# Retention's first tiles: block 1 copied and scaled a tile later, output weights' low half at tile 2, weight splits spread over more tiles

## The chip, the cores and the metric

The kernel runs on one NeuronCore of a Trainium2 chip. The metric is the device time of one execution in microseconds (us), the median over several executions; smaller is better. The core has five engines that run side by side and meet at semaphores: TensorE (PE, matrix products and transposes), VectorE (DVE), ScalarE (ACT), GpSimd (POOL) and SyncE (SP), which here only issues transfers.

## The reference

The reference is a chain of four residual blocks on x of shape (2, 2048, 256), that is 4096 rows of 256 values:

```python
x = x + _L0_attn_a_ref(_layernorm(x, axis=-1), ...)   # retention + ffn, two layers
x = x + _L0_ffn_ref(_layernorm(x, axis=-1), w_up, w_down)
x = x + _L0_attn_b_ref(_layernorm(x, axis=-1), ...)   # window attention
x = x + _L0_ffn_ref(_layernorm(x, axis=-1), w_up, w_down)
```

The change touches the first block alone, and in it the retention of each of the two layers:

```python
for i in range(L):                                     # L = 2
    Xn = _layernorm(X, ln1_w[i], ln1_b[i])
    Q = jnp.einsum('bsd,hdk->bhsk', Xn, WQ[i])
    K = jnp.einsum('bsd,hdk->bhsk', Xn, WK[i])
    V = jnp.einsum('bsd,hdk->bhsk', Xn, WV[i])
    Q = Q * cosq + _rotate_every_two(Q) * sinq
    K = K * cosk + _rotate_every_two(K) * sink
    scores = jnp.einsum('bhsk,bhtk->bhst', Q, K) * Dm[None]
    Yh = jnp.einsum('bhst,bhtk->bhsk', scores, V)
    Y = Yh.transpose(0, 2, 1, 3).reshape(B, S, H * HD)
    Y = _groupnorm(Y, gn_w[i], gn_b[i])
    G = jax.nn.silu(Xn @ WG[i])
    Y = G * Y @ WO[i] + X
    Yn = _layernorm(Y, ln2_w[i], ln2_b[i])
    X = jax.nn.silu(Yn @ ffn_w1[i] + ffn_b1[i]) @ ffn_w2[i] + ffn_b2[i] + Y
```

## The kernel before

The program is a row of stages: `retention` (layer 0), `ffn`, `retention` (layer 1), `ffn`, a ternary ffn, the window attention, and a ternary ffn. x stays in SBUF the whole time. Every product is made of fp32 halves: a matrix w is split into w_hi, a copy in fp32r that ACT makes (`high_half`, L79), and w_lo = w - w_hi, which DVE makes (`low_half`, L85), and a product is three passes (hi x hi, hi x lo, lo x hi).

`retention` works on 32 tiles n of 128 rows. Four tiles are a block b of 512 rows; blocks alternate between the two batch entries. Each engine has a body that is written out by hand, in which turn k of iteration i issues a few steps, each on another tile or block, so the order of an engine's work is the order of the code. Iteration i = 0 holds what comes ahead of the first tile; in iteration i = 1 turn k is tile n = k. The iterations 0, 1 and the last two are written out, the others are one loop. `at_start(x)` is true where x is the number 0, so `at_start(n)` is tile 0, `at_start(n - 1)` tile 1 and `at_start(n - 2)` tile 2. The argument `first` is set in layer 0 alone: there x and all weights have to be loaded first, and the input of the layer is itself normalised in place (`rows_in_place` on ACT, with scales from `scale_in_place` on POOL).

For one tile n the steps are these. TensorE makes the products for queries and keys (`project_heads`, tile pj), DVE turns them (`rotate`, L1337 and L1340), POOL adds the two parts (`rotary_sum`, L1233), TensorE transposes them (`transpose_heads`, L1783), and ACT copies that out (`heads_out`, L1567). Then come the scores (L1798), one tile later in the order; DVE masks them (`masked`, L1350), and TensorE makes the new state and the outputs (`chunk_out`, L1811 to L1822). DVE carries the state on (`next_state`, L1366 to L1371), ACT copies the outputs (`columns_out`, L1578), TensorE transposes them back, and ACT copies the rows (`rows_out`, L1585). The scores of tile n + 1 wait for all of these: for the state sum (`in_done`), for `columns_out` of tile n (`y_moved`) and for `rows_out` of tile n - 1 (`y_done`), since they share one PSUM tile, sc.

For a block the normalised rows are transposed (L1773), ACT copies them as xt and xt_hi (`inputs`, L1560), and DVE makes xt_lo (`input_low`, L1326). Of block 1 the first half of this, `inputs(1, 0, 1)` and `input_low(1, 0, 1)`, is done in tiles 1 and 2.

The weights of the ffn that follows are loaded during retention. SP issues two transfers of 1 MB into the tile staging, `loads`, with the semaphore `prefetched`. In layer 0 staging holds the layer's own weights until then, so SP first waits for all five of their low halves, of which `own_low(4)`, the output weights', is the last:

```python
                sp.wait_ge(own_lo_done, len(first["halves"]))
            prefetch(sp, loads, prefetched)
```

Eight jobs (`halves`, four for the up weights, four for the down weights) then split them: ACT makes a high half, and DVE waits for it (`hi_done`) and makes the low one. Before, both did two jobs at the end of each of the tiles 4 to 7.

Of the kernel before, what the change touches and what calls it, by code (L numbers as in the profile page):

```python
# [107 lines left out]
def at_start(idx):  # L108

    return isinstance(idx, int) and idx == 0  # L110
# [895 lines left out]
def retention(nc, name, X, ident, lane, *, qkv, gate, out_w, norm, gn, rotary, decay, group_eps, carry, state_decay,  # L1006
# [8 lines left out]
    with ExitStack() as c:  # L1015
# [98 lines left out]
        U = 2 * TB  # L1114
# [5 lines left out]

        TOTAL = NB + (next_norm is not None)

        def transposed(b, j):

            return tr[0] if first is not None and at_start(b) and j == 1 else tr[1]
# [32 lines left out]
        def _(pool):  # L1158
# [92 lines left out]
            def body(i):  # L1251
                for k in range(U):
                    n = U * i + k - AHEAD
                    if live(n, NT):
                        rotary_sum(n, k)
                    if k % TB == TB - 1 and fresh(2 * i + k // TB):
                        if not at_start(i):
                            scales(2 * i + k // TB, k // TB)
                        elif k == TB - 1:
                            first_scale(0)  # L1260
                            scale_in_place(0)
                    if at_start(n):
                        first_scale(1)
                        if first is not None:
                            scale_in_place(1)
                    if isinstance(i, int) and i == N and k == U - 1:
                        second_scale()
                    at = (k - AHEAD - 4) // 2
                    if k % 2 == 0 and live(4 * i + at, NH):
                        group_rstd(4 * i + at, at)  # L1270
                    at = (k - AHEAD - 5) // 2
                    if k % 2 == 1 and live(4 * i + at, NH):
                        gated(4 * i + at, at)
# [4 lines left out]
        def _(dve):  # L1278
# [36 lines left out]
            def aggregate(b, at):  # L1315
                at_least(dve, xn_done, b - 1)
                dve.wait_ge(stats_done, TB * (b + 1))
                apart(dve, dve_waited)
                for t in range(TB):
                    last = nc.vector.bn_aggr(mv[:, at % 2, t, :], stats[:, t, :])  # L1320
                last.then_inc(mv_done, 1)
# [138 lines left out]
            def body(i):  # L1460
                if isinstance(i, int) and i == N + 1:
                    drain(i)
                    return
                for k in range(U):
                    n = U * i + k - AHEAD
                    if first is not None and at_start(n):
                        dve.wait_ge(rotary_loaded, 16 * 2)
                    if live(n, NT):
                        rotate(n, i, k - AHEAD)
                    if first is not None and at_start(n - 1):  # L1470
                        dve.wait_ge(tables_loaded, 16 * (len(first["tables"]) - 2))
                    if live(n - 1, NT):
                        masked(n - 1, k - 1)
                    if live(n, NT):
                        values(n, k)
                    if at_start(n):
                        for t in range(TB):
                            statistics(1, 0, 1, t)
                        aggregate(1, 1)
                        if first is not None:  # L1480
                            own_low(4)
                    if at_start(n - 1):
                        first_normalise(1)
                    if k % 2 == 0:
                        at = (k - AHEAD - 4) // 2
                        if live(4 * i + at, NH):
                            square_sums(4 * i + at)
                        at = (k - AHEAD - 6) // 2
                        if live(4 * i + at, NH):
                            gated_low(4 * i + at)  # L1490
                    else:
                        at = (k - AHEAD) // TB + 1
                        if fresh(2 * i + at):
                            input_low(2 * i + at, k % TB // 2, at)
                        if first is not None and at_start(i) and k == U - 1:
                            own_low(2)
                            own_low(3)
                        at = (k - AHEAD - 7) // 2
                        if live(4 * i + at, NH):
                            residual(4 * i + at, i, at)  # L1500
                    if live(n - 1, NT):
                        next_state(n - 1, k - 1)
                    if at_start(i) and k >= TB:
                        pass
                    elif fresh(2 * i + k // TB) or (after_last(2 * i + k // TB) and i == N):
                        if k % TB < TB - 1:
                            statistics(2 * i + k // TB, i, k // TB, k % TB)
                        if k % TB == TB - 2:
                            statistics(2 * i + k // TB, i, k // TB, TB - 1)
                            aggregate(2 * i + k // TB, k // TB)  # L1510

                    if at_start(i) and k == TB - 2:
                        if first is not None:
                            first_normalise(0)
                            for j in range(2):
                                own_low(j)
                            centre_values()
                        dve.wait_ge(consts_set, 3)
                    if isinstance(i, int) and i == 1 and k >= U // 2:
                        for j in range(2 * k - U, 2 * k - U + 2):  # L1520
                            dve.wait_ge(hi_done, j + 1)
                            low_half(nc, halves[j])

# [7 lines left out]
        def _(act):  # L1531
# [116 lines left out]
            def body(i):  # L1648
# [3 lines left out]
                for k in range(U):  # L1652
                    n, t = U * i + k - AHEAD, k % TB
                    b, at = 2 * i + (k - AHEAD) // TB, (k - AHEAD) // TB
                    if live(n - 2, NT):
                        columns_out(n - 2, k - 2)
                    q = 4 * i + (k - AHEAD - 3) // 2
                    if live(n - 3, NT):
                        rows_out(n - 3, q, k - AHEAD - 3)
# [28 lines left out]
                            normed(4 * i + half)  # L1688
                    if live(n, NT):
                        heads_out(n, k)  # L1690
                    if at_start(n - 1):
                        inputs(1, 0, 1)
                    if at_start(i) and k == TB - 1 and first is not None:
                        act.wait_ge(qkv_loaded, 16)
                        own_high(0)
# [4 lines left out]
                    if first is not None and at_start(n):  # L1700
                        act.wait_ge(weights_loaded, 16 * (len(first["weights"]) - 2))
                        own_high(4)
                        act.wait_ge(tables_loaded, 16 * (len(first["tables"]) - 2))
                    if isinstance(i, int) and i == 1 and k >= U // 2:
                        if k == U // 2:
                            act.wait_ge(prefetched, 16 * len(loads))
                        for j in range(2 * k - U, 2 * k - U + 2):
                            high_half(nc, halves[j]).then_inc(hi_done, 1)

            if first is not None:  # L1710
# [1146 lines left out]
```

## Time and profile before

| | us |
|---|---|
| median of 3 timed runs | 1497.44 (1497.07 to 1497.51) |
| the profiled execution | 1497.22 |
| its span, first to last instruction | 1495.3 |
| busy: PE, DVE, ACT, POOL | 1431.2, 1035.8, 929.8, 831.9 |

The profile's page gives busy times of each engine, shares of 40 slices of the span, the transfers, the chain of work that ended last and the costliest groups of instructions. The trace behind it gives each instruction with its start, its length, the idle time of its engine before it and what ended that. All rows shown here are of the one profiled execution.

### The profile page before, as it was taken

What the parts mean: (1) busy time and instruction counts of PE and PEld (TensorE: products, weight loads), DVE (VectorE), ACT (ScalarE), POOL (GpSimd) and SP (SyncE); (2) the same over time, 40 slices, a digit from 0 to 9 for tenths busy, and PEclk for the clock granted to TensorE, in tenths of its full rate; (3) what the DMA queues carried; (4) which work ended last, traced back from release to release, by engine and by line L of the source; (5) the groups of instructions that cost most, each with busy time, mean ns of one, the idle gap of its engine ahead of it and who ended that gap; (6) DMA issues with size and microseconds to landing.
All of it is one profiled execution on the core that took longest, in us unless ns stands there. A gap on an engine that the chain in (4) does not pass through costs nothing. (4 is left out here: it accounts for less than half of the span.)

```text
span 1495.3 us, 36363 instructions
## 1 busy us (share of the span) xinstructions
PE 1431.2 (96%) x13034; PEld 1188.7 (79%) x13066; DVE 1035.8 (69%) x2284; ACT 929.8 (62%) x1748; POOL 831.9 (56%) x915
## 2 busy tenths in 40 slices
PE   5999999999998999999999999997999999989998
PEld 4777878899986788878999888885777777768886
DVE  6878777564537877885755678665777777756774
ACT  4665565565544555555655567775777777758775
POOL 3665766411204676573824457766666676636674
PEclk9999999999999999999999999999999999999999
DMA  7000000100001000000210010000000000000101
GB/s 250 2 2 1 0 2 2 36 1 1 1 15 44 2 2 0 1 1 34 95 29 15 1 40 2 0 1 1 2 1 0 0 0 0 0 2 1 42 30 43
DMA packets 21143, 26.27 MB, mean 18 GB/s; under 512 B 1952, under 2 KB 19104, under 8 KB 20896
## 3 DMA queue, kind: packets, MB, share of 16 engines
q1 hardware_dynamic: 20736, 24.61, 5.0%
q8 instruction: 75, 1.23, 0.3%
q14 instruction: 44, 0.36, 0.1%
q10 hardware_dynamic: 288, 0.07, 0.0%
HBM read 20.48 MB, written 4.19 MB: 17 GB/s over the span
## 5 line engine op out<-in xcount | busy, mean ns | idle before, releaser
L547 DVE TENSOR_TENSOR ffn_h_lo<-ffn_h,ffn_h_hi 128x512 fp32r<-128x512 f32 x112 | 86.2, 770 | 122.2 <-ACT ffn_h_hi L754 122.2
L753 ACT ACTIVATE ffn_h<-ffn_hp,c_b 128x512 f32<-128x512 f32 x112 | 77.2, 689 | 145.3 <-PE ffn_hp L850 144.8
L547 DVE TENSOR_TENSOR ternary_ffn_h_lo<-ternary_ffn_h,ternary_ffn_h_hi 128x512 fp32r<-128x512 f32 x128 | 110.8, 866 | 76.0 <-ACT ternary_ffn_h_hi L754 75.7
L1233 POOL TENSOR_TENSOR ret_qk<-ret_qk,ret_qk_sin 128x512 f32<-128x512 f32 x64 | 82.7, 1292 | 103.2 <-DVE ret_qk_sin L1340 102.6
L861 PE MATMUL ternary_ffn_yp<-down_ternary,ternary_ffn_h_hi 128*128 128x256 f32 x512 | 132.3, 291 | 0.0
L1239 POOL TENSOR_TENSOR ret_rstd<-ret_sums,ret_minus_half 128x16 f32<-128x16 f32 x32 | 103.7, 3240 | 42.7 <-DVE ret_sums L1382 42.7
L861 PE MATMUL ffn_yp<-down_hi,ffn_h_hi 128*128 128x256 f32 x448 | 127.4, 284 | 0.0
L861 PE MATMUL ternary_ffn_yp<-down_ternary,ternary_ffn_h_lo 128*128 128x256 f32 x512 | 127.4, 280 | 0.0
L861 PE MATMUL ffn_yp<-down_hi,ffn_h_lo 128*128 128x256 f32 x448 | 125.0, 279 | 0.0
L861 PE MATMUL ffn_yp<-down_lo,ffn_h_hi 128*128 128x256 f32 x448 | 124.9, 279 | 0.0
L443 POOL TENSOR_TENSOR ternary_ffn_h_sq<-ternary_ffn_h_sq 128x512 f32<-128x512 f32 x61 | 94.6, 1560 | 41.9 <-ACT ternary_ffn_h_sq L760 38.2
L2179 POOL TENSOR_TENSOR win_rms<-win_rms,win_minus_half 128x20 f32<-128x20 f32 x31 | 115.3, 3718 | 2.6
L2403 ACT ACTIVATE wa_probs_t<-wa_tp 128x512 f32<-128x512 f32 x128 | 76.4, 597 | 62.7 <-PE wa_tp L2580 62.2
L753 ACT ACTIVATE ternary_ffn_h<-ternary_ffn_hp 128x512 f32<-128x512 f32 x128 | 76.5, 597 | 54.1 <-PE ternary_ffn_hp L850 47.8
L850 PE MATMUL ternary_ffn_hp<-xt_hi,up_ternary 128*128 128x512 f32 x256 | 102.4, 400 | 4.7 <-DVEq L730 4.4
L861 PEld LDWEIGHTS ternary_ffn_yp<-down_ternary,ternary_ffn_h_hi 128*128 128x128 f32 x512 | 96.4, 188 | 7.3 <-issue 3.8
L850 PE MATMUL ternary_ffn_hp<-xt_lo,up_ternary 128*128 128x512 f32 x256 | 101.6, 397 | 0.0
L861 PEld LDWEIGHTS ternary_ffn_yp<-down_ternary,ternary_ffn_h_lo 128*128 128x128 f32 x512 | 96.6, 189 | 3.1
L1337 DVE TENSOR_TENSOR ret_qk<-ret_pj,rotary 128x512 f32<-128x512 f32 x64 | 44.2, 690 | 68.7 <-PE ret_pj L1729 68.7
L850 PE MATMUL ffn_hp<-xt_hi,up_hi 128*128 128x512 f32 x224 | 88.9, 397 | 2.4 <-DVEq L730 2.4
L850 PE MATMUL ffn_hp<-xt_lo,up_hi 128*128 128x512 f32 x224 | 88.9, 397 | 0.0
L1350 DVE TENSOR_TENSOR ret_probs<-ret_sc,causal 128x1024 f32<-128x1024 f32 x64 | 78.3, 1224 | 15.0 <-issue 10.9
(322 smaller groups left out, 4700.2 us busy)
## 6 DMA issues: line engine op xcount, KB each, us to landing
staging<-in_w SPq DMA_DIRECT2D x4, 1024.0 KB, 7.0
ffn_x_in<-in_x SPq DMA_DIRECT2D x8, 512.0 KB, 3.9
X<-in_x SPq DMA_DIRECT2D x7, 512.0 KB, 7.9
out<-X SPq DMA_DIRECT2D x7, 512.0 KB, 2.9
staging<-in_wqkv SPq DMA_DIRECT2D x2, 768.0 KB, 5.7
rotary<-in_rotary SPq DMA_DIRECT2D x1, 1024.0 KB, 7.3
staging<-in_w_up SPq DMA_DIRECT2D x1, 1024.0 KB, 5.0
staging<-in_w_down SPq DMA_DIRECT2D x1, 1024.0 KB, 7.5
```

The source lines that it names most:

```text
L443: nc.gpsimd.tensor_tensor(h_sq[:, m, :], h_sq[:, m, :], h_sq[:, m + 1, :], ALU.add).then_inc(sq_added, 1)
L547: nc.vector.tensor_tensor(h_lo[:, m % R, :], h[:, m % R, :], h_hi[:, m % R, :].bitcast(F32), ALU.subtract).then_inc(h_ready, 1)
L753: nc.scalar.activation(h[:, m % R, :], hp[m % 2][:, :], fn, bias=bias)
L850: last = nc.tensor.matmul(hp[m % 2][:, :], w[:, j, m * P:(m + 1) * P], x[:, k, j, :], start=(n == 0), stop=(n == len(todo) - 1))
L861: last = nc.tensor.matmul(yp[k][t // 2][:, (t % 2) * D:(t % 2 + 1) * D], x[:, m % R, t * P:(t + 1) * P], w[:, m, :], start=(m == 0 and t % ...
L1233: nc.gpsimd.tensor_tensor(qk[:, r, :, :, :], qk[:, r, :, :, :], qk_sin[:, r, :, :, :], ALU.add).then_inc(qk_done, 1)
L1239: nc.gpsimd.tensor_tensor(rstd[:, :], sums[:, 1, :], minus_half[:, :], ALU.pow).then_inc(rstd_done, 1)
L1337: nc.vector.tensor_tensor(qk[:, r, :, :, :], src, cos, ALU.mult)
L1350: nc.vector.tensor_tensor(pr[:, at % 2, :, :, :], sc[:, :, 0:HT].rearrange("p h (j n) -> p h j n", j=NG), causal[:, :].unsqueeze(1).unsque ...
L2179: nc.gpsimd.tensor_tensor(rms[:, 1, :], rms[:, 0, :], minus_half[:, :], ALU.pow).then_inc(rms_work, 1)
L2403: nc.scalar.activation(pt[:, g, :, :].rearrange("p c n -> p (c n)"), tp[:, :], ACT.Copy).then_inc(pt_done, 1)
```

## The change

Three edits, all in `retention`, and all in the written-out iteration i = 1 (tiles 0 to 7):

1. `scale_in_place(1)` on POOL goes from tile 0 to tile 1, behind the rotary sum; `inputs(1, 0, 1)` on ACT goes from the end of tile 1 to tile 2, behind `columns_out(0)`; `input_low(1, 0, 1)` on DVE goes from tile 1 to tile 2, behind the values.
2. `own_low(4)` on DVE goes from tile 0 to tile 2, behind that `input_low`.
3. The eight jobs are spread by `split_at`: in layer 0 two at tile 2, one each at 3 and 4, two at 5, one each at 6 and 7; in layer 1 one at each of the tiles 0 to 7.

The steps of TensorE and SP keep their order.

```diff
+        def split_at(k):
+
+            if first is None:
+                return (k,)
+            return {2: (0, 1), 3: (2,), 4: (3,), 5: (4, 5), 6: (6,), 7: (7,)}.get(k, ())
...
                     if at_start(n):
                         first_scale(1)
-                        if first is not None:
-                            scale_in_place(1)
+                    if at_start(n - 1) and first is not None:
+                        scale_in_place(1)
...
-                        if first is not None:
-                            own_low(4)
                     if at_start(n - 1):
                         first_normalise(1)
+                    if at_start(n - 2):
+                        input_low(1, 0, 1)
+                        if first is not None:
+                            own_low(4)
...
-                        if fresh(2 * i + at):
+                        if fresh(2 * i + at) and not at_start(n - 1):
                             input_low(2 * i + at, k % TB // 2, at)
...
-                    if isinstance(i, int) and i == 1 and k >= U // 2:
-                        for j in range(2 * k - U, 2 * k - U + 2):
+                    if isinstance(i, int) and i == 1:
+                        for j in split_at(k):
                             dve.wait_ge(hi_done, j + 1)
                             low_half(nc, halves[j])
...
                         columns_out(n - 2, k - 2)
+                    if at_start(n - 2):
+                        inputs(1, 0, 1)
...
-                    if at_start(n - 1):
-                        inputs(1, 0, 1)
...
-                    if isinstance(i, int) and i == 1 and k >= U // 2:
-                        if k == U // 2:
+                    if isinstance(i, int) and i == 1:
+                        if split_at(k) and split_at(k)[0] == 0:
                             act.wait_ge(prefetched, 16 * len(loads))
-                        for j in range(2 * k - U, 2 * k - U + 2):
+                        for j in split_at(k):
                             high_half(nc, halves[j]).then_inc(hi_done, 1)
```

In the pieces of each engine's order below, the line numbers of the changed kernel are 6 (DVE) and 8 (ACT) higher. DVE in layer 0, from the end of tile 0 to the rotation of tile 2, before:

```order
L85 TENSOR_TENSOR out_w_lo<-staging,out_w_hi 128x512 [waits ret0_own_hi_done]
L1312 BN_STATS ret_stats<-X 128x6 [waits ret0_x_loaded2,ret0_mv_done]
L1337 TENSOR_TENSOR ret_qk<-ret_pj,rotary 128x512 [waits ret0_qk_full]
L1340 TENSOR_TENSOR ret_qk_sin<-ret_pj,rotary 128x256 x2
L1350 TENSOR_TENSOR ret_probs<-ret_sc,causal 128x1024 [waits ret0_v_full,ret0_sc_full,ret0_tables_loaded]
L1358 TENSOR_TENSOR ret_v<-ret_sc,decay 128x256 [waits ret0_v_full]
L1406 TENSOR_SCALAR xn<-X,mean_var,ret_scale 128x256 [waits ret0_tp_full,ret0_first_scaled]
L1406 TENSOR_SCALAR xn<-X,mean_var,ret_scale 128x256 x3
L1326 TENSOR_TENSOR xt_lo<-xt,xt_hi 128x512 [waits ret0_xt_read]
L1366 TENSOR_TENSOR ret_state_in<-ret_sc,ret_own_state 128x64 [waits ret0_kv_full]
```

and in the changed kernel, DVE of layer 0 from the mask of tile 2's turn (that of tile 1) to the rotation of tile 3:

```order
L1356 TENSOR_TENSOR ret_probs<-ret_sc,causal 128x1024 [waits ret0_v_full,ret0_sc_full]
L1364 TENSOR_TENSOR ret_v<-ret_sc,decay 128x256 [waits ret0_y_full,ret0_v_full]
L1332 TENSOR_TENSOR xt_lo<-xt,xt_hi 128x512 [waits ret0_xt_read]
L85 TENSOR_TENSOR out_w_lo<-staging,out_w_hi 128x512 [waits ret0_own_hi_done]
L1372 TENSOR_TENSOR ret_state_in<-ret_sc,ret_own_state 128x64 [waits ret0_state_done,ret0_kv_full]
L1375 TENSOR_TENSOR ret_own_state<-ret_state_in,carry 128x64 [waits ret0_in_done]
L1377 TENSOR_TENSOR ret_state<-ret_state_in,state_decay 128x256
L1318 BN_STATS ret_stats<-X 128x6 x2
L1326 BN_AGGR mean_var<-ret_stats 128x2 [waits ret0_xn_done,ret0_stats_done]
L85 TENSOR_TENSOR up_lo<-staging,up_hi 128x512 [waits ret0_hi_done] x2
L1343 TENSOR_TENSOR ret_qk<-ret_pj,rotary 128x512 [waits ret0_kv_full,ret0_qk_full]
```

xt_lo and out_w_lo have moved behind the values of tile 2, and two low halves of the up weights stand ahead of the rotation of tile 3. ACT of layer 0 in the changed kernel, from the gates of tile 2 to the copy of the next inputs:

```order
L1581 ACTIVATE ret_gate<-ret_pj 128x512 [waits ret0_g_full]
L1575 ACTIVATE ret_qkt<-ret_tr 128x512 [waits ret0_y_full,ret0_tq_full]
L79 ACTIVATE up_hi<-staging 128x512 [waits ret0_prefetched]
L79 ACTIVATE up_hi<-staging 128x512
L1586 ACTIVATE ret_y_cols<-ret_sc 128x256 [waits ret0_y_full]
L1593 ACTIVATE ret_y<-ret_sc 128x256 [waits ret0_back_full]
```

Before, the two rows of up_hi stood two tiles further on, behind the copy of tile 4's heads, and with them the wait for prefetched. DVE of layer 1 in the changed kernel, at the end of tile 0 (hi_done is the count of high halves):

```order
L85 TENSOR_TENSOR up_lo<-staging,up_hi 128x512 [waits ret0_hi_done]
L1343 TENSOR_TENSOR ret_qk<-ret_pj,rotary 128x512 [waits ret0_pool_waited]
L1346 TENSOR_TENSOR ret_qk_sin<-ret_pj,rotary 128x256 x2
```

The low half stands ahead of the rotation of tile 1, where nothing stood before. (Layer 1 uses the semaphores of layer 0 again under other meanings, and the order prints the first name that each had.)

## Rows read from the trace of the kernel before

**Rows 1.** The page, part 1: busy us, share, instructions of each engine.

```profile
PE 1431.2 (96%) x13034; PEld 1188.7 (79%) x13066; DVE 1035.8 (69%) x2284; ACT 929.8 (62%) x1748; POOL 831.9 (56%) x915
```

**Rows 2.** Timeline of PE, layer 0: start, length, instruction [idle before, releaser].

```profile
20.99 0.39 PE L1729 MATMUL ret_pj<-qkv_hi,xt_lo 128*128 128x512 f32 x1
...
25.05 0.66 PE L1783 MATMUL ret_tr<-c_ident,ret_qk 128*128 128x128 f32 x4 [2.11 <-POOL ret_qk L1233]
...
30.26 0.73 PE L1798 MATMUL ret_sc<-ret_qkt 32*128 32x128 f32 x16 [1.08 <-DVE ret_state_in L1366]
...
31.61 0.28 PE L1729 MATMUL ret_sc<-qkv_hi,xt_lo 128*128 128x256 f32 x1
...
37.56 0.73 PE L1798 MATMUL ret_sc<-ret_qkt 32*128 32x128 f32 x16
...
40.42 0.66 PE L1783 MATMUL ret_tr<-c_ident,ret_qk 128*128 128x128 f32 x4 [1.24 <-POOL ret_qk L1233]
```

**Rows 3.** Timeline of DVE and POOL, layer 0, tiles 0 to 2.

```profile
21.16 0.69 DVE L85 TENSOR_TENSOR out_w_lo<-staging,out_w_hi 128x512 fp32r<-128x512 f32 x1 [1.11 <-ACT out_w_hi L79]
...
22.11 0.67 DVE L1337 TENSOR_TENSOR ret_qk<-ret_pj,rotary 128x512 f32<-128x512 f32 x1
...
29.29 0.69 DVE L1326 TENSOR_TENSOR xt_lo<-xt,xt_hi 128x512 fp32r<-128x512 f32 x1 [3.10 <-ACT xt_hi L1560]
...
32.22 1.22 DVE L1350 TENSOR_TENSOR ret_probs<-ret_sc,causal 128x1024 f32<-128x1024 f32 x1
33.35 0.41 DVE L1358 TENSOR_TENSOR ret_v<-ret_sc,decay 128x256 f32<-128x256 f32 x1
...
23.73 1.27 POOL L1233 TENSOR_TENSOR ret_qk<-ret_qk,ret_qk_sin 128x512 f32<-128x512 f32 x1
32.38 1.29 POOL L1233 TENSOR_TENSOR ret_qk<-ret_qk,ret_qk_sin 128x512 f32<-128x512 f32 x1 [7.38 <-DVE ret_qk_sin L1340]
```

**Rows 4.** Timeline of DVE, layer 0: the rotation of tile 3.

```profile
37.67 0.69 DVE L1337 TENSOR_TENSOR ret_qk<-ret_pj,rotary 128x512 f32<-128x512 f32 x1 [0.95 <-PE ret_pj L1729]
```

**Rows 5.** Timelines of DVE and PE, layer 1, tiles 1 and 2.

```profile
452.31 0.69 DVE L1337 TENSOR_TENSOR ret_qk<-ret_pj,rotary 128x512 f32<-128x512 f32 x1 [0.89 <-PE ret_pj L1729]
...
453.55 0.28 PE L1729 MATMUL ret_sc<-qkv_hi,xt_lo 128*128 128x256 f32 x1
455.06 0.66 PE L1783 MATMUL ret_tr<-c_ident,ret_qk 128*128 128x128 f32 x4 [1.23 <-POOL ret_qk L1233]
...
460.27 0.73 PE L1798 MATMUL ret_sc<-ret_qkt 32*128 32x128 f32 x16 [1.08 <-DVE ret_state_in L1366]
```

**Rows 6.** SP's issues, and issue to landing of the second load, layers 0 and 1.

```profile
21.88 0.89 SPq L68 DMA_DIRECT2D staging<-in_w  x2
...
DMA to landing us min/median/max: 8.8/8.8/8.8
...
445.55 0.88 SPq L68 DMA_DIRECT2D staging<-in_w  x2
...
DMA to landing us min/median/max: 7.5/7.5/7.5
```

**Rows 7.** Timeline of ACT, layer 0.

```profile
35.92 0.39 ACT L1578 ACTIVATE ret_y_cols<-ret_sc 128x256 f32<-128x256 f32 x1 [0.91 <-PE ret_sc L1822]
...
48.92 1.14 ACT L79 ACTIVATE up_hi<-staging 128x512 fp32r<-128x512 f32 x2
```

**Rows 8.** PE at the window stage; a slice: length, busy PE, PEld, DVE, ACT, POOL, clock.

```profile
1021.10 0.45 PE L2529 MATMUL wa_tr<-c_ident,win_padded 128*128 128x128 f32 x1 [3.83 <-DVEq L2213]
...
1021.00:1024.00 3.00, 2.90 (x11) 2.74 (x11) 1.90 (x5) 2.14 (x4) 0.98 (x4) 0.50 0.03 5
```

**Rows 9.** Timelines of POOL and PE at the end of tile 7.

```profile
67.15 1.29 POOL L1233 TENSOR_TENSOR ret_qk<-ret_qk,ret_qk_sin 128x512 f32<-128x512 f32 x1 [0.43 <-DVE ret_qk_sin L1340]
...
76.59 0.65 PE L1773 MATMUL ret_tr<-c_ident,xn 128*128 128x128 f32 x4 [1.23 <-ACT xn L1536]
...
505.97 0.65 PE L1773 MATMUL ret_tr<-c_ident,xn 128*128 128x128 f32 x4 [0.62 <-ACT xn L1536]
```

More of the change, by code:

```diff
@@ L1479, in body @@
                         aggregate(1, 1)
+                    if at_start(n - 1):
+                        first_normalise(1)
+                    if at_start(n - 2):
+                        input_low(1, 0, 1)
                         if first is not None:
                             own_low(4)
-                    if at_start(n - 1):
-                        first_normalise(1)
                     if k % 2 == 0:
@@ L1690, in body @@
                         heads_out(n, k)
-                    if at_start(n - 1):
-                        inputs(1, 0, 1)
                     if at_start(i) and k == TB - 1 and first is not None:
```

## The prediction

> **What bounds the kernel now.** I read the page first, then the timelines of the four engines, TensorE's first, through the first tiles of each retention layer, since only there does the change act. The page shows TensorE busy for 96% of the span [rows 1]; so the end is set by TensorE's own queue: a microsecond of its idle time that is removed or added stays until the end, unless it is given back at a later wait. TensorE's waits in layer 0's first tiles are few: for the rotary sum on POOL (2.11 us in tile 1, 1.24 in tile 3), and once for DVE's state sum, 1.08 us at the scores of tile 1 [rows 2]. These are what the change can win. What it can lose is the slack of ACT and DVE: both work in order, so one wait at a tile's end holds everything of the next tile.
>
> I call the layers 0 and 1, tiles n = 0, 1, 2, and "scores(n)" and so on by the names of the code. A start at 37.56 means us from the span's start.
>
> **Part 1, layer 0: the output weights' low half (own_low(4)) leaves tile 0.** Before, DVE waited 1.11 us for ACT's copy and then spent 0.69 us on it; rotate(1) could only start at 22.11, and POOL's sum, behind scale_in_place(1), started at 23.73 [rows 3]. The product that rotate(1) reads ended at 21.38 (20.99 + 0.39). A clean rotate starts about 0.04 us after its product, and takes 2.75 us to the transposes of its heads: 37.67 to 40.42 in tile 3, 452.31 to 455.06 in layer 1 [rows 2, 4, 5]. With scale_in_place(1) put behind POOL's sum, the transposes of tile 1 start at 21.42 + 2.75 = 24.17 instead of 25.05 [rows 2]: 0.88 us won. DVE has no work of another kind to put in that hole, so nothing replaces it. scale_in_place(1) now runs behind that sum, where POOL stood idle for 7.38 us [rows 3], and ACT asks for its result only behind the inputs' copy: hidden.
>
> **Part 2, both layers: input_low(1, 0) moves to tile 2, behind the values.** DVE stood 3.10 us at it, with the state sum behind, and TensorE's scores(1) waited 1.08 us for that sum [rows 2, 3]. Now the state sum runs before, and the inputs' copy on ACT runs behind columns_out(0), which the same scores need. Won: 1.08 us in each layer. The low half itself (0.69 us) lies in DVE's slack ahead of the state sum of tile 1, and nothing reads it before tile 4.
>
> So far layer 0 is 1.96 us ahead: scores(2) could start at 37.56 - 1.96 = 35.60 [rows 2].
>
> **Part 3, layer 0: the weight splits start at tile 2, but their loads now start later.** This is the term that decides. SP issues the two loads of 1 MB when the fifth low half is done (it overwrites the same staging tile). Before, that was at 21.88, right behind own_low(4) [rows 3, 6]. Now own_low(4) stands behind the mask, the values and input_low(1, 0) of tile 2. The values' product ends at 31.61 + 0.28 - 1.96 = 29.93 [rows 2]; the mask then takes 1.22, the values 0.41, the two low halves 0.69 each [rows 3], with about 0.1 us of overlap at each handover: 32.8. The second load is issued 0.4 us later, at 33.2. Its time to landing was 8.8 us here, right behind the blocks of x, and 7.5 us in layer 1 with the queue empty [rows 6]. At tile 2 the queue is empty, so I take 7.5 and keep 8.8 as the upper bound: landed at 40.8 (42.1).
>
> ACT now waits for that at the end of tile 2, from about 33.0, where before it asked at 48.92, long after the landing [rows 7]. Behind the wait on ACT stand the two high halves (1.14), columns_out(1) (0.39) and rows_out(0) (0.4) [rows 7], and TensorE's scores(2) wait for both of the last: 40.8 + 1.9 - 0.1 = 42.6 instead of 35.6. TensorE stands for 7.0 us. DVE stands too: its low halves 0 and 1 wait for the high halves, the last ends at 42.7, and only then comes rotate(3), which was at 37.67 [rows 4]. Its transposes follow at 42.7 + 2.75 = 45.4, against 40.42: 5.0 us late.
>
> **The clock after such a stand.** At the start of the window stage TensorE was idle for 3.83 us, and the granted clock was 0.50 right after, that is 1.2 instead of 2.4 GHz, over the 3 us from 1021 to 1024 [rows 8]. A stand of 7.0 us is longer. So scores(2) and the values' product of tile 3, 1.6 us of work at full clock, take about 2.8; the mask of tile 2 starts at 45.4 and ends at 46.6, and chunk_out(2), which came 0.6 us behind the transposes at 41.0 before, starts at 46.65. The step at tile 2 is +5.6 us with the low clock, +5.0 without.
> The Trainium skill (TensorE: Matmul & The Clock Gate, Part 1) says that an idle array falls back to 1.2 GHz and returns to 2.4 GHz after sustained work; by that rule the trace agrees, and the larger of the two values stands.
>
> A weighing of the load itself: the second load ended 7.9 us after the first was issued in layer 1 [rows 6].
> The Trainium skill (DMA: Bandwidth & Descriptors, Rules for kernel authors) wants a transfer issued early and waited for late, which is what this change undoes; its fit in Anatomy of one DMA (2.0 us and the bytes at 436 GB/s, given there for another issuing path) would give an estimate of 6.8 us for both loads, and the sum would be 1.1 us lower by it.
>
> **Part 4, layer 1: the first half at tile 0.** Here the loads are issued at 445.55 when the layer starts, and the second lands at 445.55 + 0.4 + 7.5 = 453.5 [rows 6]. ACT now waits for it behind heads_out(0); that costs ACT nothing, its next step waits for the transposes of tile 1. But DVE's low_half(0) stands ahead of rotate(1): high half to 454.1, low half to 454.8, and rotate(1) starts then instead of at 452.31 [rows 5]: +2.5 us for the transposes of tile 1 (455.06). Part 2 gives 1.08 back at scores(1) (460.27) [rows 5]. Left: +1.4 us.
>
> **Part 5, the splits at one per tile.** In tiles 4 to 7 DVE and ACT carry half of what they did where one split stands for two. TensorE waits for none of them, so most of it is worth nothing. One place counts: POOL's sum of tile 7 waited 0.43 us for a rotate that came behind two low halves, and TensorE's transposes of the following block waited 1.23 us (layer 0) and 0.62 us (layer 1) for a chain that runs through that sum [rows 9]. I take 0.4 us in each layer; bounds 0 and 0.6.
>
> **The sum.** Layer 0: +5.6 - 0.4 = +5.2. Layer 1: +1.4 - 0.4 = +1.0. Together +6.2 us. The profiled execution took 1497.2 us (span 1495.3), 0.2 us below the median of 1497.4 of the timed runs. 1497.4 + 6.2 = **1503.6 us**. A measurement of this kernel tells about 0.2% from no change, 3.0 us.
>
> **The rivals.**
> 1. *The second stand also lowers the clock.* In layer 1 TensorE would be idle from 453.83 to 457.55, 3.7 us; the row that shows a fall had 3.83, and the 2.11 us in layer 0 brought none: the transposes behind it took 0.66 us as in tile 3 [rows 2]. Three us at 0.50 are 1.5 us of work lost [rows 8], nearly all of it on the path: 1505.1 us.
> 2. *The loads land as slowly as before (8.8 us):* +1.3, 1504.9 us. For it: the same two transfers once took that. Against: x is all in by then.
> 3. *The clock stays up, or ACT's chain is a little shorter:* 1503.0 us.
> 4. *Later slack gives half of it back.* TensorE's remaining waits in the layers are for chains that hang on TensorE's own work and shift with it, which speaks against: 1500.5 us.
> 5. *Not slower: ACT's wait is hidden.* If the loads had landed when ACT asks, layer 0 would keep its 1.96 and 0.4 us, with layer 1 at +1.0: 1496.1 us. The point from which it decides: columns_out(1) is due on ACT at 35.92 - 1.96 = 33.96 [rows 7], less 1.14 for the high halves, so the landing has to come by 32.8, the moment of its issue. No load of 1 MB landed in under 5.0 us. Were the wait of layer 1 hidden as well, 1493.6 us.
>
> **How the numbers follow.** Forecast 0.52, rival 1 0.20, rival 2 0.10, rival 3 0.08, rival 4 0.06, rival 5 0.04 (of which 0.02 with both waits hidden). The range: rivals 1 and 2 together would be 1503.6 + 1.5 + 1.3 = 1506.4; below, rival 3 and the bound of 0.6 in part 5 with 1 us less of load give 1501.6. Low 1501.6, high 1506.5. Slower by over 0.2% (above 1500.4): everything but half of rival 4, and rival 5: 0.93. Within 0.2%: 0.05. Faster: 0.02.
>
> **What would show it.** Right: ACT's up_hi in layer 0 starts near 40.8 with some 7 us of idle time before it, released by the DMA; scores(2) start near 42.6 with a wait for ACT's ret_y; the granted clock is 0.5 in the three us that follow; the scores(1) rows have no wait for ret_state_in in either layer; the first transposes of tile 1 are near 24.2 and 457.5. Wrong: up_hi starts before 36, or scores(2) near 35.6; or tile 8 of layer 0 is less than 4 us later than before.

## The result and the profile after

| | before, us | changed, us |
|---|---|---|
| median of 5 timed runs | 1497.07 (1495.22 to 1497.51) | 1504.94 (1503.05 to 1506.66) |
| the profiled execution | 1497.22 | 1506.66 |
| its span | 1495.3 | 1504.9 |

The ratio is 1.0051, with an interval of 1.0039 to 1.0062: the changed kernel is slower. The median moved by 7.9 us (1504.94 - 1497.07), the span of the two profiled executions by 9.6 (1504.9 - 1495.3). Beside [rows 1], the page of the changed kernel has the same instructions in the same number, but for matmul records that one trace or the other lost:

```profile
PE 1441.4 (96%) x13066; PEld 1195.2 (79%) x13066; DVE 1036.4 (69%) x2284; ACT 930.9 (62%) x1748; POOL 829.8 (55%) x915
```

DVE, ACT and POOL are as busy as before. TensorE's busy time is 10.2 us larger with the same work (before, 32 matmul records are missing): matmuls that ran at the lower clock are longer ones. The line numbers of the changed kernel are 6 (DVE, POOL) and 8 (ACT, PE) higher than before.

**The waits.** TensorE's three longest groups of waits, on the page's trace (waits for: us in total, times, longest):

```profile
PE ret_tr L1781 <- DVE xn L1412: 9.1, 1, 9.1
PE ret_tr L1791 <- POOL ret_qk L1239: 8.5, 6, 3.6
PE ret_sc L1806 <- ACT ret_y L1593: 8.3, 3, 7.2
```

The first is the kernel's start and stands in both (9.9 us before). The third is new: the scores wait for ACT, once for 7.2 us. The longest of the second group, 3.6 us, is new too and lies in layer 1.

**Layer 0.** TensorE's timeline, answering to [rows 2]:

```profile
23.29 0.66 PE L1791 MATMUL ret_tr<-c_ident,ret_qk 128*128 128x128 f32 x4 [1.23 <-POOL ret_qk L1239]
...
30.66 0.60 PE L1791 MATMUL ret_tr<-c_ident,ret_qk 128*128 128x128 f32 x4
...
41.68 1.24 PE L1806 MATMUL ret_sc<-ret_qkt 32*128 32x128 f32 x16 [7.17 <-ACT ret_y L1593]
...
44.46 1.11 PE L1791 MATMUL ret_tr<-c_ident,ret_qk 128*128 128x128 f32 x4
...
54.78 0.60 PE L1791 MATMUL ret_tr<-c_ident,ret_qk 128*128 128x128 f32 x4
```

The wait at tile 1's transposes fell from 2.11 to 1.23 us, the wait for ret_state_in at its scores is gone, and in their place scores(2) stand for 7.17 us. Why is on SP's, ACT's and DVE's timelines, one after the other:

```profile
31.88 0.89 SPq L68 DMA_DIRECT2D staging<-in_w  x2
```

```profile
39.84 1.15 ACT L79 ACTIVATE up_hi<-staging 128x512 fp32r<-128x512 f32 x2 [7.95 <-DMA staging<-in_w]
40.89 0.36 ACT L1586 ACTIVATE ret_y_cols<-ret_sc 128x256 f32<-128x256 f32 x1
41.16 0.37 ACT L1593 ACTIVATE ret_y<-ret_sc 128x256 f32<-128x256 f32 x1
```

```profile
40.50 1.29 DVE L85 TENSOR_TENSOR up_lo<-staging,up_hi 128x512 fp32r<-128x512 f32 x2 [6.73 <-ACT up_hi L79]
41.71 0.68 DVE L1343 TENSOR_TENSOR ret_qk<-ret_pj,rotary 128x512 f32<-128x512 f32 x1
```

SP issues the two loads of 1 MB at 31.9, ten microseconds later than in [rows 6]; ACT asks for them at the end of tile 2 and stands for 7.95 us until the second has landed. The columns of tile 1 and the rows of tile 0 on ACT, for which the scores of tile 2 wait, and the rotation of tile 3 on DVE are queued behind the splits.

**Layer 1.** TensorE's, ACT's and DVE's timelines, answering to [rows 5]:

```profile
464.07 0.94 PE L1791 MATMUL ret_tr<-c_ident,ret_qk 128*128 128x128 f32 x4 [3.65 <-POOL ret_qk L1239]
...
469.56 0.73 PE L1806 MATMUL ret_sc<-ret_qkt 32*128 32x128 f32 x16
```

```profile
460.06 0.63 ACT L79 ACTIVATE up_hi<-staging 128x512 fp32r<-128x512 f32 x1 [1.95 <-DMA staging<-in_w]
```

```profile
460.72 0.69 DVE L85 TENSOR_TENSOR up_lo<-staging,up_hi 128x512 fp32r<-128x512 f32 x1 [2.68 <-ACT up_hi L79]
461.33 0.68 DVE L1343 TENSOR_TENSOR ret_qk<-ret_pj,rotary 128x512 f32<-128x512 f32 x1
```

The wait for ret_state_in is gone here too, but ACT waits 1.95 us for the load, rotate(1) runs behind the low half of the first split, and the transposes of tile 1 stand for 3.65 us.

**The clock.** Slices of TensorE's granted clock in the changed kernel, around the two stands (length of the slice, busy time of PE, PEld, DVE, ACT, POOL with their counts, then the clock as a share of 2.4 GHz, DMA share, GB/s):

```profile
34.00:38.00 4.00, 0.51 (x3) 0.07 (x1) 0.00 (x0) 0.00 (x0) 0.00 (x0) 0.95 1.04 398
38.00:45.00 7.00, 3.32 (x25) 2.87 (x26) 2.97 (x6) 3.03 (x6) 1.69 (x3) 0.50 0.18 58
45.00:46.00 1.00, 0.71 (x13) 0.31 (x15) 1.00 (x2) 0.39 (x1) 0.93 (x1) 0.50 0.00 0
46.00:51.00 5.00, 5.00 (x43) 3.84 (x42) 2.04 (x6) 2.95 (x7) 1.30 (x3) 0.50 0.00 0
51.00:52.00 1.00, 1.00 (x18) 0.53 (x16) 0.42 (x1) 1.00 (x3) 0.00 (x0) 0.85 0.00 0
...
464.00:468.00 4.00, 3.93 (x45) 2.89 (x45) 3.14 (x10) 1.50 (x3) 0.02 (x1) 0.57 0.00 0
```

It fell to 1.2 GHz during the first stand, and was back only in the slice from 51 to 52, some 9.6 us after the scores had started (41.68). In layer 1 it fell as well, to 0.57 on average over four microseconds.

**Where the time went.** Start of the transposes of a tile's heads on TensorE, counted from those of the layer's tile 0 (the changed kernel's layer 0 started 0.89 us earlier, at 18.43 against 19.32, which is no effect of the change: the same start lies between 18.4 and 19.3 over the profiled executions of all runs here). The columns "late" are the differences:

| | before | changed | late, us |
|---|---|---|---|
| layer 0, tile 1 | 5.73 | 4.86 | -0.87 |
| tile 2 | 14.40 | 12.23 | -2.17 |
| tile 3 | 21.10 | 26.03 | +4.93 |
| tile 4 | 28.23 | 36.35 | +8.12 |
| tile 8 | 57.76 | 65.25 | +7.49 |
| layer 1, tile 1 | 4.85 | 7.25 | +2.40 |
| tile 2 | 13.52 | 16.05 | +2.53 |
| tile 8 | 56.25 | 58.12 | +1.87 |

Together +7.49 + 1.87 - 0.89 = +8.5 of the 9.6 us; the rest is at the starts of later stages, which the change doesn't touch (last section).

### The profile page after: what moved, and what is told of

It is laid out like the page before. It is cut to its first block and busy times, and to the rows that moved or that the text cites. A ratio compares the mean times of both kernels' runs of the same rounds, so it can differ in the third digit from the quotient of the medians.

```text
span 1504.9 us, 36395 instructions
## 1 busy us (share of the span) xinstructions
PE 1441.4 (96%) x13066; PEld 1195.2 (79%) x13066; DVE 1036.4 (69%) x2284; ACT 930.9 (62%) x1748; POOL 829.8 (55%) x915
## 3 DMA queue, kind: packets, MB, share of 16 engines
q8 instruction: 75, 1.23, 0.3%
```

## The experiments

Each was timed beside the kernel before on the same chip. The kernel before had a median of 1498.51 us beside the first four, and 1498.19 beside the next four. The ratio is estimated from all of these runs and differs from the quotient of the two medians by up to 0.0006, 0.9 us. The edits are shown against the changed kernel. "Late" is used as in the table above, and "early" for the opposite.

**Both other edits, the splits where they were.** Edits 1 and 2 of the change alone (the copies a tile on, own_low(4) at tile 2); all splits from tile 4 in both layers:

```
         def split_at(k):
 
-            if first is None:
-                return (k,)
-            return {2: (0, 1), 3: (2,), 4: (3,), 5: (4, 5), 6: (6,), 7: (7,)}.get(k, ())
+            return {4: (0, 1), 5: (2, 3), 6: (4, 5), 7: (6, 7)}.get(k, ())
```

> Edits 1 and 2 alone: both layers' splits two per tile from tile 4 as before. Theory: 1.96 us won in layer 0 and 1.08 us in layer 1, nothing lost: 3.0 us under the kernel before, 1494.0 us. Rival (the late loads or the moved copies cost something): same as before or slower.

Measured: 1494.53 us, ratio 0.9973 (0.9963 to 0.9982): faster. Tile 8 of layer 0 is 2.26 us early, tile 2 of layer 1 1.30 us early, and the scores of tile 2 don't wait. TensorE's timeline:

```profile
34.50 0.73 PE L1804 MATMUL ret_sc<-ret_qkt 32*128 32x128 f32 x16
37.35 0.66 PE L1789 MATMUL ret_tr<-c_ident,ret_qk 128*128 128x128 f32 x4 [1.23 <-POOL ret_qk L1237]
```

So the gains of the first two edits are real, and all of the loss belongs to the early splits or to their meeting with edit 2. The loads are issued late here as well, at 31.94; nobody asks for them before 45.85, when they are long in.

**Layer 0's splits late, layer 1's early.**

```
             if first is None:
                 return (k,)
-            return {2: (0, 1), 3: (2,), 4: (3,), 5: (4, 5), 6: (6,), 7: (7,)}.get(k, ())
+            return {4: (0, 1), 5: (2, 3), 6: (4, 5), 7: (6, 7)}.get(k, ())
```

> The change, but with layer 0's splits two per tile from tile 4 as before; own_low(4) stays in tile 2, so the loads stay late (issued near 32, landing near 40). Theory: nobody asks for them before tile 4's end near 45, so layer 0 wins its 1.96 us and no stand is left; layer 1 +2.1 us as in the change, near 1497.2 us. Rival (late loads cost in themselves, through SP or the queue): layer 0 stays slower, 1500 us or more.

Measured: 1497.1 us, 0.9995 (0.9986 to 1.0004). Layer 0 keeps its gain though its loads are issued at 32.09: tile 8 is 2.27 us early, so late loads that nobody asks for cost nothing there. Tile 2 of layer 1 is 3.39 us late, against 2.53 in the changed kernel's first profile: the clock was low there from about 454.2 to 461.0, twice as long as in the changed kernel.

**Layer 1's splits late, layer 0's early.**

```
             if first is None:
-                return (k,)
+                return {4: (0, 1), 5: (2, 3), 6: (4, 5), 7: (6, 7)}.get(k, ())
```

> The change, but with layer 1's splits two per tile from tile 4 as before. Theory: layer 1's stand of 3.65 us goes and its low clock with it, and 1.08 us are won there against the kernel before; layer 0 keeps its loss. About 3.3 us under the change: 1501.6 us. Rival (layer 1's low half ahead of rotate(1) is hidden): within 1 us of the change.

Measured: 1502.17 us, 1.0025 (1.0015 to 1.0035). Against both late, layer 0's early splits cost 1502.17 - 1494.53 = 7.6 us and layer 1's 1497.1 - 1494.53 = 2.6 us. The two costs stand apart, in the layers where the theory puts them. With the 4.0 us that splits_late wins (1498.51 - 1494.53) they make +6.2 us; the changed kernel's interval was +5.8 to +9.3 us (1.0039 to 1.0062).

**The same early splits, with the loads issued early.** Only own_low(4) goes back into tile 0:

```
                         aggregate(1, 1)
+                        if first is not None:
+                            own_low(4)
                     if at_start(n - 1):
                         first_normalise(1)
                     if at_start(n - 2):
                         input_low(1, 0, 1)
-                        if first is not None:
-                            own_low(4)
```

> The change, but with the output weights' low half (own_low(4)) back in tile 0; the splits stay spread from tile 2 (layer 0) and tile 0 (layer 1). Theory (the loads): SP issues the two loads near 21 again, they land near 30, before ACT asks near 32, so ACT has no wait, TensorE no stand and no low clock in layer 0. Layer 0 then keeps the 1.08 us at scores(1), some 0.2 us at tile 1 and 0.5 us at tile 8; layer 1 stays about 2.1 us slower than before. Together near 1497.4 us, 7 us under the change. Rival (the work): the high and low halves ahead of columns_out and of rotate in tiles 2 and 3 cost by themselves; then at least half of the loss of layer 0 stays, 1501 us or more.

Measured: 1498.85 us, 0.9997 (0.9988 to 1.0007), on the same chip and in the same runs as split1_late. The stand in layer 0 is gone although its splits are at tile 2, as in the change. SP's timeline, then ACT's, then TensorE's:

```profile
21.15 0.89 SPq L68 DMA_DIRECT2D staging<-in_w  x2
```

```profile
32.59 1.14 ACT L79 ACTIVATE up_hi<-staging 128x512 fp32r<-128x512 f32 x2
```

```profile
24.11 0.66 PE L1791 MATMUL ret_tr<-c_ident,ret_qk 128*128 128x128 f32 x4 [1.90 <-POOL ret_qk L1239]
...
35.24 0.73 PE L1806 MATMUL ret_sc<-ret_qkt 32*128 32x128 f32 x16
```

ACT finds the data there (the second load is issued at 21.6 and takes 8.1 us) and doesn't wait; scores(2) don't either. Tile 8 of layer 0 is 2.05 us early. What remains is layer 1's loss: tile 2 there is 2.72 us late. That settles the cause in layer 0: not the splits at tile 2, but their meeting with loads that edit 2 had put off by 10 us.

**Edit 1 alone** (the next block's rows a tile on; own_low(4) in tile 0, splits from tile 4).

> Edit 1 alone: scale_in_place(1), inputs(1, 0) and input_low(1, 0) moved, own_low(4) in tile 0 and the splits in tiles 4 to 7 as before. Theory: 1.08 us won in each layer at scores(1), and 0.2 us at tile 1 of layer 0, where POOL's sum no longer stands behind scale_in_place(1): 2.4 us under the kernel before, 0.6 us above edits 1 and 2 together. Rival (the 0.88 us at tile 1 belongs to POOL's order and not to own_low(4)): the same as edits 1 and 2 together.

Measured: 1496.49 us, 0.9985 (0.9976 to 0.9994); the medians differ by 1.7 us. Tile 1 of layer 0 is 0.21 us early, against 0.88 in splits_late, so the other 0.67 us belong to own_low(4) and the rival is out. (By time alone it isn't: the interval overlaps that of splits_late.) The gain at tile 2 of layer 0 can't be read from this profile: TensorE waited 1.96 us at the transposes of tile 1, the clock was at 0.50 from about 25.8 to 29.2, and tile 2 is neither early nor late. In layer 1, tile 2 is 1.31 us early (463.31 - 451.10 against 13.52).

**Keeping the clock up during the stand.** 27 products of 128x512 that nobody reads, ahead of the scores of tile 2, behind a wait that lets them start when the stand begins:

```
+                    if at_start(n - 3) and first is not None:
+                        pe.wait_ge(tq_done, 3)
+                        for _ in range(27):
+                            nc.tensor.matmul(tr[0][:, :], xt_hi[:, 0, 0, 0:P], qkv[0][:, 0, 0:2 * D], start=True, stop=True)
                     if live(n - 1, NT):
                         scores(n - 1, k - 1)
```

> The change, and during layer 0's stand TensorE makes 27 products of 128x512 that nobody reads (some 6.4 us of work, into the PSUM tile that the next head transposes overwrite), ahead of scores(2). Theory (the clock): the stand keeps its length and its wait for ACT, but the granted clock stays 1.00 behind it, so the transposes of tile 4 come 5.0 us late instead of 8.1, and the time falls by about 3 us under the change. Rival (the loss behind the stand is the chain DVE, POOL, ACT and not the clock): within 0.5 us of the change.

Measured: 1504.17 us, 1.0038 (1.0024 to 1.0052), single runs from 1501.04 to 1506.61. The profile shows what was meant: the clock stays at 1.00 and the scores take 0.73 us instead of 1.24, so that tile 4 is 4.82 us late, not 8.12. Slices, then TensorE:

```profile
34.00:38.00 4.00, 4.00 (x19) 3.22 (x18) 0.00 (x0) 0.00 (x0) 0.00 (x0) 1.00 1.03 392
38.00:45.00 7.00, 5.12 (x46) 3.76 (x47) 4.26 (x8) 3.04 (x6) 1.73 (x4) 1.00 0.17 55
```

```profile
41.57 0.73 PE L1806 MATMUL ret_sc<-ret_qkt 32*128 32x128 f32 x16 [0.73 <-ACT ret_y L1593]
```

The stand alone therefore costs its 4.8 us at tile 4 and after; what is above that is the clock. In time the gain is not shown: the interval takes in the lower part of the changed kernel's (1.0039 to 1.0062).

**The same in both layers**, with 12 such products ahead of the transposes of tile 1 in layer 1.

> As the run before, and 12 more such products (2.8 us) in layer 1 ahead of the head transposes of tile 1. Theory: the 3.65 us stand of layer 1 stays, its low clock goes; layer 1 is then 1.4 us slower than before instead of 2.5 (by the tile starts), 1.1 us under the run before.

Measured: 1502.28 us, 1.0027 (1.0018 to 1.0035). In layer 1 the clock stayed at 1.00, and tile 2 is 1.14 us late instead of 2.53: the stand without the clock. The interval lies below the whole of the changed kernel's (1.0039 to 1.0062, each beside the kernel before on its own chip): in time too, part of the loss is the clock. How much is left open, for in layer 0 the clock fell all the same, though TensorE had worked through the stand and since then never waited for more than 1.15 us. TensorE's waits there:

```profile
41.90 0.73 PE L1806 MATMUL ret_sc<-ret_qkt 32*128 32x128 f32 x16 [0.81 <-ACT ret_y L1593]
44.68 1.12 PE L1791 MATMUL ret_tr<-c_ident,ret_qk 128*128 128x128 f32 x4 [1.15 <-POOL ret_qk L1239]
```

and two of its slices:

```profile
45.00:46.00 1.00, 1.00 (x20) 0.67 (x18) 0.78 (x2) 0.16 (x1) 0.90 (x2) 0.50 0.00 0
46.00:51.00 5.00, 5.00 (x42) 3.71 (x32) 1.40 (x4) 3.31 (x8) 1.91 (x3) 0.50 0.00 0
```

warm_layer0 has the same instructions in layer 0 and nearly the same waits there (0.73 and 1.14 us), and its clock stayed at 1.00. I had no theory that expects this fall, and have none now.

**The splits as far apart as the loads allow.** From this, a version: edits 1 and 2 as they are, layer 0's first split at tile 4, layer 1's at tile 1:

```
             if first is None:
-                return (k,)
-            return {2: (0, 1), 3: (2,), 4: (3,), 5: (4, 5), 6: (6,), 7: (7,)}.get(k, ())
+                return {1: (0,), 2: (1,), 3: (2,), 4: (3,), 5: (4, 5), 6: (6,), 7: (7,)}.get(k, ())
+            return {4: (0, 1, 2), 5: (3, 4), 6: (5,), 7: (6, 7)}.get(k, ())
```

> Edits 1 and 2, and the splits spread where the loads have landed: layer 0 three at tile 4, two at 5, one at 6, two at 7; layer 1 one each at tiles 1 to 4, two at 5, one each at 6 and 7. Theory: no stand in either layer, and the single split at tile 6 gives back 0.4 to 0.5 us at tile 8 in each layer: 3.8 us under the kernel before, 0.8 us under edits 1 and 2 alone. Rival (three at tile 4 push ACT's copies into scores(5), or the gain at tile 8 is taken by the next wait there): no better than edits 1 and 2 alone.

Measured: 1493.76 us (1490.91 to 1494.14), 0.9964 (0.9951 to 0.9977): faster than the kernel before and the changed one. Its interval overlaps that of splits_late (0.9963 to 0.9982), so that the spreading in itself is worth anything is not shown in time. In the profile tile 8 is 0.37 us earlier than in splits_late in layer 0 (2.63 against 2.26 early) and 0.62 in layer 1 (1.98 against 1.36), as part 5 of the prediction has it.

**How long the low clock lasts.** In the first profiles of the change and of split1_late the stand was nearly the same (7.17 and 7.04 us; tile 3 is 4.93 and 4.73 us late), but tile 4 was 8.12 us late in one and 5.55 in the other. So two more executions of each were profiled.

> The changed kernel, one more execution. In its first profile the granted clock stayed at 0.50 from the stand to 51.2 us and tile 4 of layer 0 began 8.1 us late against tile 0; in split1_late, with the same layer 0, it was back by 45.2 us and tile 4 was only 5.5 us late. Theory (the stand is fixed, the length of the low clock behind it is settled anew in every execution): tile 3 again 4.9 to 5.0 us late, tile 4 either about 5.5 or about 8.1 us late, and over four looks both are seen. Rival (the length belongs to the kernel): 8.1 us in every look at this kernel.

> As changed_look2. Theory: tile 3 4.9 to 5.0 us late, tile 4 about 5.5 or about 8.1. Rival: 8.1. In layer 1 tile 2 is 2.5 us late where the clock falls behind the stand of 3.7 us, and 1.4 where it doesn't; my theory expects the fall in most looks, not in all.

> Split1_late (layer 1's splits from tile 4, layer 0 as in the change), one more execution. Theory: tile 3 of layer 0 4.9 to 5.0 us late, tile 4 about 5.5 or about 8.1. Rival (the length belongs to the kernel): 5.5 again.

> As split1_late_look2. Theory: tile 4 about 5.5 or about 8.1 us late. Rival: 5.5.

Measured, with the time of that execution (one execution of the kernel before took 1500.19 us on this chip):

| execution | us | tile 3 late | tile 4 late |
|---|---|---|---|
| changed_look2 | 1504.85 | +4.82 | +5.63 |
| changed_look3 | 1507.96 | +4.75 | +8.13 |
| split1_late_look2 | 1500.42 | +4.80 | +5.61 |
| split1_late_look3 | 1500.53 | +4.88 | +5.69 |

Slices of changed_look2 and then of changed_look3:

```profile
38.00:45.00 7.00, 2.62 (x22) 2.33 (x22) 2.56 (x5) 3.03 (x6) 1.16 (x1) 0.61 0.30 99
45.00:46.00 1.00, 1.00 (x5) 0.72 (x4) 0.71 (x1) 0.00 (x0) 0.75 (x4) 0.50 0.00 0
46.00:51.00 5.00, 4.72 (x66) 3.40 (x65) 3.82 (x10) 3.89 (x9) 2.01 (x3) 0.97 0.00 0
```

```profile
38.00:45.00 7.00, 2.64 (x22) 2.33 (x22) 2.56 (x5) 3.03 (x6) 1.18 (x1) 0.56 0.30 96
45.00:46.00 1.00, 1.00 (x5) 0.72 (x4) 0.72 (x1) 0.00 (x0) 0.75 (x4) 0.50 0.00 0
46.00:51.00 5.00, 4.71 (x44) 3.45 (x43) 2.73 (x7) 2.65 (x6) 1.99 (x3) 0.50 0.00 0
```

The two executions do the same work up to 46 us; then one is at full clock and does 66 matmuls in five microseconds, the other stays at 0.50 and does 44. They differ by 3.1 us in time, and by 2.5 at tile 4. That the length belongs to the kernel falls: the changed kernel showed both. It doesn't follow the length of the stand either: the two long falls came behind stands of 7.17 and 7.01 us, the four short ones behind 7.04 to 7.20. One thing differs before the return: the clock fell at about 39.5 us in changed_look2 and at 38.8 in changed_look3, and it came back at 46.3 and 52.5. What settles the length isn't in the trace. The Trainium skill (TensorE: Matmul & The Clock Gate, Part 1) says that the hardware's watch on the array isn't tied to the kernel's start, so that the same kernel sees its clock change at other places in each run, by half a microsecond either way. The fall of these two executions agrees with that; their return, 6.2 us apart, differs by more than the page gives. The stand was some 0.1 us shorter than I had expected for these executions (tile 3 4.75 to 4.88 us late against 4.9 to 5.0). In layer 1 the clock fell in all three profiles of the changed kernel.

## Why the prediction was right

The forecast was 1503.6 us in a range of 1501.6 to 1506.5; the median is 1504.94. As a change, +6.2 us were forecast and +7.9 came. Sign and mechanism hold; the size fell short in the two terms that hang on the clock, as the steps below show; the profiled execution, 1506.66 us, in which layer 0 has the longer fall, lies just above the range. By its steps, the first profile of the changed kernel beside them:

| step | predicted | measured |
|---|---|---|
| part 1, tile 1 of layer 0 | -0.88 | -0.87 |
| parts 1 and 2, tile 2 | -1.96 | -2.17 |
| part 3, time to landing of the second load | 7.5 | 7.5 |
| idle time of scores(2) | 7.0 | 7.17 |
| tile 3 | +5.0 | +4.93 |
| the clock, tile 4 | +5.6 | +8.12, or +5.63 |
| part 5, from tile 4 to tile 8 | -0.4 | -0.63 |
| layer 0 in all | +5.2 | +7.49, or +5.01 |
| part 4, tile 1 of layer 1 | +2.5 | +2.40 |
| tile 2 of layer 1 | +1.4 | +2.53 |
| part 5, to tile 8 of layer 1 | -0.4 | -0.66 |

- **Parts 1 and 2** hold as priced (the 0.2 us more at tile 2 I haven't followed up); splits_late measures them together at 4.0 us (1498.51 - 1494.53). Its profile has 2.26 + 1.30 = 3.6 of it.
- **Part 3** holds in each link: issue, landing, ACT, DVE, TensorE. The landing answers to the row of [rows 6] for layer 1 (7.5), not to that for layer 0 (8.8): rival 2 is out. The query of SP's line over layer 0 gives, for the two loads:

```profile
DMA to landing us min/median/max: 5.0/6.3/7.5
```

- **The clock after the stand of layer 0** is a term with two values. The 3 us at 0.50 of [rows 8] were one example of a fall, and I took it for the length of any. The changed kernel had +5.63 once and +8.12 and +8.13 in the other two profiles; split1_late had +5.55 to +5.69 in its three. In the first profile the term was mis-sized, 3.2 us (8.12 - 4.93) in place of 0.6; in changed_look2 it was 0.8, and tile 8 came at 82.03, 5.01 us late (82.03 - 19.26 - 57.76) where +5.2 was forecast. So the close agreement in layer 0 is partly luck: it holds in the execution with the shorter fall only.
- **Part 4** is where the sum fell short: the stand of 3.65 us did lower the clock. This is rival 1, given 0.20, and it deserved more, since [rows 8] had a fall behind a wait of just 3.83. It cost what warm_both took away: 2.53 - 1.14 = 1.4 us, against the 1.5 that rival 1 gave. Its 1505.1 us lie by the median.
- **Rivals 3 and 4** are out: the clock fell, and nothing of the stand was given back, but for part 5. **Rival 5** is what own_low_tile0 builds: the loads early enough, and layer 0 keeps its gain.

By the changed kernel's three profiles the sum is then +5.0 in layer 0 at the shorter fall, +7.5 at the longer, and +1.9 to +2.1 in layer 1: 6.9 to 9.6 us, and the 7.9 of the medians lie within.

## What to carry to other kernels

A step that is moved takes with it everything it stands in front of, and here that was a DMA issue: own_low(4) freed a buffer, and putting it two tiles on started a load of 8 us ten microseconds later, while the other part of the same change asked for it seventeen microseconds earlier (31.9 against 48.9). In layer 0 each of the two is harmless without the other: tile 8 is 2.26 us early without the early splits and 2.05 us early with the early loads. (Layer 1's early splits cost 2.6 us by themselves.) So ask of each pair of edits what they do to one transfer's issue and its first use. And where a wait would be new on TensorE, price it at its length and then at the clock, at more than one length of the fall.

## What the runs showed of the hardware

**After a stand the clock is low for a length that varies, and a short stand lowers it in some executions and not in others.** Behind the stand of 7.0 to 7.2 us in layer 0 the clock was at 0.50 for 6.8 us in one execution of the changed kernel (39.5 to 46.3) and for about 13.6 us in the two others. Whether a short stand lowers it at all differs too: the first product of the ternary layer waits 2.37 us in both kernels, for a semaphore that DVE's sequencer (DVEq) raises at the start of the stage. TensorE before the change, and its slice:

```profile
871.92 0.50 PE L850 MATMUL ternary_ffn_hp<-xt_hi,up_ternary 128*128 128x512 f32 x1 [2.37 <-DVEq L730]
```

```profile
872.00:880.00 8.00, 7.64 (x43) 6.35 (x44) 5.35 (x16) 7.80 (x15) 5.47 (x9) 1.00 0.53 182
```

and the same in the changed kernel:

```profile
880.28 0.51 PE L850 MATMUL ternary_ffn_hp<-xt_hi,up_ternary 128*128 128x512 f32 x1 [2.37 <-DVEq L730]
```

```profile
880.00:888.00 8.00, 7.72 (x37) 6.53 (x37) 4.74 (x11) 7.34 (x13) 4.68 (x11) 0.79 0.57 182
```

The same wait, and a clock of 1.00 in one and 0.79 in the other. A fall came behind a shorter wait too: 1.96 us in tile 1 of copies_only, while 2.11 us at the same place in the kernel before and 1.90 in own_low_tile0 brought none. Such falls in later stages are probably what the tiles leave of the 9.6 us; I have not taken them out one by one.

**Runs of one kernel differ with the clock.** The 30 timed runs of the kernel before beside the first four experiments lay between 1495.85 us, at a mean clock of 0.997, and 1500.61, at 0.991. The 13 runs at 0.996 or 0.997 took 1495.85 to 1498.68 us, the five at 0.991 took 1499.35 to 1500.61. This is a correlation; no run changes the clock alone. A single execution lay up to 2.7 us below or 2.1 us above the median of 1498.51, so a comparison of 0.1% needs many runs. The profiled execution of the kernel before has 0.997, the changed kernel's 0.988.

**The clock can fall without a stand.** In warm_both it did so near 44.3 us, within TensorE's wait of 1.15 us (43.5 to 44.7) and some 2.4 us after one of 0.81; otherwise it had worked without a stop for more than ten microseconds. The Trainium skill (TensorE: Matmul & The Clock Gate, Part 1) tells of falls behind long idle stretches, and of another kernel in which the clock kept falling and returning because the array idled briefly, but often, between its groups of matmuls. The fall of warm_both may be of the second kind, but no run here tests that, and warm_layer0 with the same work had no fall. What sets it off stays open.
